# Pairwise attention scores of a four-layer graph network: ring blocks shared among three engines as a maximum

## The reference, cut to what matters

```python
s1 = jnp.einsum('bkf,ef->bke', x, W1)
s2 = jnp.einsum('bkf,ef->bke', x, W2)
pre = s1[:, :, None, :] + s2[:, None, :, :] + b_lin
h = jnp.where(pre >= 0, pre, ALPHA * pre)          # ALPHA = 0.2
e = jnp.einsum('bije,e->bij', h, a) + bias
attn = softmax(e, axis=2)
out = sigmoid(jnp.einsum('bij,bjf->bif', attn, x))
```

## Time and profile before

| | before |
|---|---|
| median of 3 executions | 6323.53 us |
| lowest, highest | 6313.05, 6334.41 us |
| span of the profiled execution | 6243.5 us |
| time of the profiled execution beside its span | not given by the page; the median is 80.0 us above the span |
| TensorE matmuls, weight loads busy | 5979.7, 2282.0 us |
| VectorE busy | 5954.0 us |
| ScalarE busy | 6039.2 us |
| GpSimd busy | 305.3 us |

### The profile page before, as it was taken

How to read it: one execution, slowest core, us unless ns; L and a number is a source line. 1 busy time by engine, 2 the same in 40 slices (tenths; PEclk the granted TensorE clock), 3 DMA queues, 4 the chain that set the end, 5 groups by cost and what they waited for, 6 DMA issues and landing times.

```text
span 6243.5 us, 130456 instructions
## 1 busy us (share of the span) xinstructions
PE 5979.7 (96%) x41684; PEld 2282.0 (37%) x41684; DVE 5954.0 (95%) x22159; ACT 6039.2 (97%) x15993; POOL 305.3 (5%) x646
## 2 busy tenths in 40 slices
PE   8899999999999999999999999999999999999997
PEld 2233333333333333333333333333333333333334
DVE  9999999999999999999999999999999999999993
ACT  8999999999999999999999999999999999999993
POOL 0000000000000000000000000000000000000000
PEclk9999999999999999999999999999999999999998
DMA  0000000000000000000000000000000000000000
GB/s 12 3 4 7 7 6 3 6 7 7 6 3 7 6 7 7 6 3 6 7 7 6 3 7 6 7 7 2 7 6 7 7 6 3 7 6 7 6 4 6
DMA packets 44317, 36.24 MB, mean 6 GB/s; under 512 B 4721, under 2 KB 39410, under 8 KB 43506
## 3 DMA queue, kind: packets, MB, share of 16 engines
q1 hardware_dynamic: 43506, 26.50, 1.4%
HBM read 9.71 MB, written 8.39 MB: 3 GB/s over the span
## 4 chain that ended last, share of the span: by engine, by line
PE 48%; ACT 41%; DVE 9%; issue 2%; POOL 1%; DMA 0%; SPq 0%; ACTq 0%; DVEq 0%; POOLq 0%
ACT ring L711 34%; PE S L912 26%; PE R L856 8%; DVE ring L514 7%; PE S L856 4%; PE V L856 3%; PE PA L856 1%; PE R L1054 1%; ACT h L753 1%; ACT cand L824 1%; ACT tz L821 1%; PE S L903 1%; PE S L906 1%; PE R L1062 1%; ACT mT L815 1%
## 5 line engine op out<-in xcount | busy, mean ns | idle before, releaser
L711 ACT ACTIVATE ring<-V,U 128x256 f32<-128x256 f32 x13472 | 5443.3, 963 | 1.3 <-DVE G L488 1.3
L514 DVE TENSOR_SCALAR ring<-V,U 128x256 f32<-128x256 f32 x19296 | 5199.2, 345 | 24.7 <-PE S L912 21.3
L912 PE MATMUL S<-ring,a_window 128*32 128x512 f32 x32768 | 3814.0, 598 | 80.3 <-ACT ring L711 52.9
L912 PEld LDWEIGHTS S<-ring,a_window 128*32 128x32 f32 x32768 | 934.7, 110 | 2432.6 <-issue 2189.1
L856 PE MATMUL R<-mT,W 128*128 128x512 f32 (+1 forms) x640 | 338.9, 611 | 2.7 <-ACT mT L815 2.7
L416 POOL TENSOR_TENSOR minus_mean<-mv,minus_one 128x4 f32<-128x4 f32 (+1 forms) x160 | 44.4, 278 | 5852.6 <-DVE mv L535 3216.6
L856 PE MATMUL R<-AT,h 128*128 128x256 f32 x1260 | 316.7, 395 | 2.7 <-ACT h L827 2.1
L856 PEld LDWEIGHTS R<-AT,h 128*128 128x128 f32 x1260 | 230.2, 193 | 129.9 <-issue 82.2
L419 POOL TENSOR_TENSOR rstd<-var,minus_half 128x4 f32<-128x4 f32 (+1 forms) x160 | 186.7, 1167 | 12.5
L856 PEld LDWEIGHTS R<-mT,W 128*128 128x128 f32 x640 | 109.2, 189 | 205.0 <-issue 181.4
L648 DVE SCALAR_TENSOR_TENSOR rh<-tr,h3T 128x512 f32<-128x512 f32 (+1 forms) x165 | 110.8, 672 | 70.4 <-ACT tr L818 70.4
(11 more groups left out here) (178 smaller groups left out, 4371.8 us busy)
## 6 DMA issues: line engine op xcount, KB each, us to landing
X<-in_x SPq DMA_DIRECT2D x64, 128.0 KB, 2.1
X_held<-X SPq DMA_DIRECT2D x32, 256.0 KB, 2.3
out<-OUT SPq DMA_DIRECT2D x64, 128.0 KB, 1.9
raw<-in_L_gnn_w_w SPq DMA_DIRECT2D x3, 128.0 KB
A<-in_adj SPq DMA_DIRECT2D x1, 256.0 KB, 2.7
Wn<-in_L_gnn_Wn SPq DMA_DIRECT2D x1, 128.0 KB
Wm<-in_L_gnn_Wm SPq DMA_DIRECT2D x1, 128.0 KB
rawu<-in_L_gnn_u_w SPq DMA_DIRECT2D x2, 64.0 KB
```

Of the source, the lines that this page charges most:

```text
L514: block_ = dve.tensor_scalar(ring[:, place, g, half * N:(half + 1) * N], V[:, y, c], U[:, y, c, i:i + 1], 0.0, ALU.add, ALU.max)
L711: last = act.activation(ring[:, place, g, half * N:(half + 1) * N], V_bank[y][:, c * N:(c + 1) * N], ACT.Relu, bias=U[:, y, c, i:i + 1])
L912: last = pe.matmul(S[y][g * ROWS:(g + 1) * ROWS, :], a_window[:, c, ROWS - 1 - row:2 * ROWS - 1 - row], ring[:, place, g], start=False, st ...
```

## The change

The rectified sum is written as a maximum. With `w = -v`, `relu(u + v) = max(u, w) - w`. VectorE and GpSimd make `max(W, U)`, ScalarE `relu(U - W)` as before with a scale of -1. Where a block was made as a maximum, the missing `-w = v` is linear, and goes into the opening matmul's weights, which now differ by column of the weights according to who makes the block.

- `AT_minus` is the negated projection matrix. The second projection now gives `W`, in a bank and a tile of that name.
- A block of VectorE is a tensor-scalar with a single `max` (line 586 of the changed kernel).
- GpSimd makes blocks too, `min` with the largest fp32 number and then `max` with the pointer, from the same `W` and `U` into the same ring (line 488). It waits for `freed` of the place as the others do, and raises `by_pool`, for which TensorE waits as a third semaphore per lot. It steps a semaphore `pool_begun` once per lot for which nobody waits.
- `share_blocks` splits a lot three ways, with 2.63, 3.57 and 4.5 for a block of VectorE, ScalarE and GpSimd, and with 20 on GpSimd for each layer norm. Per turn this gives 433 blocks to VectorE, 288 to GpSimd and 303 to ScalarE, where it was 603, 0 and 421; times 32: 13856, 9216 and 9696, where it was 19296, 0 and 13472.
- At the start GpSimd fills a mask `by_max` (one memset of 1024 columns, 75 small ones), VectorE makes from it the weights `lin_w` with two operations. The opening matmul has one weight matrix per half of the nodes: two of 256 columns in the place of one of 512.

```diff
-VECTOR_BLOCK, SCALAR_BLOCK = 2.63, 3.62
+VECTOR_BLOCK, SCALAR_BLOCK, POOL_BLOCK = 2.63, 3.57, 4.5
+LARGEST = 3.4028234e38
...
-        n = min(range(1, BLOCKS), key=lambda n: max(v + (BLOCKS - n) * VECTOR_BLOCK, s + n * SCALAR_BLOCK))
-        shares.append(n)
-        v += (BLOCKS - n) * VECTOR_BLOCK + vector[t]
-        s += n * SCALAR_BLOCK + scalar[t]
+        def ends(share):
+            d, g, a = share
+            return sorted((v + d * VECTOR_BLOCK, q + g * POOL_BLOCK, s + a * SCALAR_BLOCK), reverse=True)
+
+        d, g, a = min(((d, BLOCKS - d - a, a) for d in range(1, BLOCKS) for a in range(1, BLOCKS - d)), key=ends)
+        shares.append((d, g, a))
+        v += d * VECTOR_BLOCK + vector[t]
+        q += g * POOL_BLOCK + pool[t]
+        s += a * SCALAR_BLOCK + scalar[t]
...
+            gp.memset(by_max[:], 1.0).then_inc(mask_ones, 1)
+            gp.wait_ge(mask_ones, 1)
+            for y in range(2):
+                for c in range(EC):
+                    for n in range(BLOCKS):
+                        g, half = group_half(n)
+                        for first, end in scalar_runs(y, c, n):
+                            last = gp.memset(by_max[:, c, y, half, g * ROWS + first:g * ROWS + end], 0.0)
+            last.then_inc(mask_set, 1)
...
+            def blocks(turn, t):
+                y, p = divmod(t, LOTS_B)
+                row, c = divmod(p, EC)
+                place, rnd = t % RING, t // RING
+                d, count, _ = SHARES[t]
+
+                if p == 0:
+                    gp.wait_ge(u_ready, turn.at(2, y + 1))
+                    gp.wait_ge(w_ready, turn.at(2, y + 1))
+                need(gp, freed[place], turn.at(ROUNDS, rnd))
+                gp.sem_inc(pool_begun, 1)
+                for n in range(d, d + count):
+                    g, half = group_half(n)
+                    i = node(t, n)
+                    last = gp.tensor_scalar(ring[:, place, g, half * N:(half + 1) * N], W[:, y, c], LARGEST,
+                                            U[:, y, c, i:i + 1], ALU.min, ALU.max)
+                last.then_inc(by_pool[place], 1)
...
                 for t in range(LOTS):
                     y, p = divmod(t, LOTS_B)
+                    if turn.has_main:
+                        blocks(turn, t)
...
-                block_ = dve.tensor_scalar(ring[:, place, g, half * N:(half + 1) * N], V[:, y, c],
-                                           U[:, y, c, i:i + 1], 0.0, ALU.add, ALU.max)
+                block_ = dve.tensor_scalar(ring[:, place, g, half * N:(half + 1) * N], W[:, y, c],
+                                           U[:, y, c, i:i + 1], None, ALU.max)
...
-                    last = act.activation(ring[:, place, g, half * N:(half + 1) * N], V_bank[y][:, c * N:(c + 1) * N], ACT.Relu,
-                                          bias=U[:, y, c, i:i + 1])
+                    last = act.activation(ring[:, place, g, half * N:(half + 1) * N], W_bank[y][:, c * N:(c + 1) * N], ACT.Relu,
+                                          bias=U[:, y, c, i:i + 1], scale=-1.0)
...
-                    pe.matmul(S[y][:].rearrange("p (r j) -> p r j", r=NB), w2_lin_wide[:],
-                              H0T[:, y].unsqueeze(1).to_broadcast([P, NB, N]), start=True, stop=False,
-                              skip_group_check=True)
+                    for r in range(NB):
+                        pe.matmul(S[y][:, r * N:(r + 1) * N], lin_w[:, y, r], H0T[:, y], start=r == 0, stop=False,
+                                  skip_group_check=True)
...
                 pe.wait_ge(by_act[place], turn.at(ROUNDS, rnd + 1))
+                pe.wait_ge(by_pool[place], turn.at(ROUNDS, rnd + 1))
```

More of the change, by code:

```diff
@@ L90, in stage_costs @@
         put(scalar, PRE, half, norm=5, copy=2.6, evacuate=12)
+        put(pool, PRE, half, stats=20)
     for ln in (LN1, LN2, LN3):
@@ L134, with group_half, node, scalar_runs @@
 SPARE_BLOCKS = spare_blocks()
+def group_half(n):
+    return divmod(n, NB)
+def node(t, n):
+    row = t % LOTS_B // EC
+    g, half = group_half(n)
+    return half * P + g * ROWS + row
+def scalar_runs(y, c, n):
+    mine = [n >= BLOCKS - SHARES[y * LOTS_B + row * EC + c][2] for row in range(ROWS)]
+    edges = [row for row in range(ROWS) if mine[row] and (row == 0 or not mine[row - 1])]
+    ends = [row + 1 for row in range(ROWS) if mine[row] and (row == ROWS - 1 or not mine[row + 1])]
+    return list(zip(edges, ends))
 def gnn_stack(nc, x, adj, L0_b, L0_a, L1_Wi, L1_bi, L1_We, L1_be, L1_Wn, L1_bn, L1_Wm, L1_bm, L2_q, L2_k, L2_v,
@@ L297, in gnn_stack @@
         by_act = [sem(f"by_act{n}") for n in range(RING)]
+        by_pool = [sem(f"by_pool{n}") for n in range(RING)]
+        mask_ones, mask_set, pool_begun = sem("mask_ones"), sem("mask_set"), sem("pool_begun")
         freed = [sem(f"freed{n}") for n in range(RING)]
@@ L508, in one_block @@
                     return
[L509 removed]
+                t = lot["t"]
+                y, p = divmod(t, LOTS_B)
                 row, c = divmod(p, EC)
[L511 to L515 removed]
+                place = t % RING
+                g, half = group_half(lot["done"])
+                i = node(t, lot["done"])
+                block_ = dve.tensor_scalar(ring[:, place, g, half * N:(half + 1) * N], W[:, y, c],
+                                           U[:, y, c, i:i + 1], None, ALU.max)
                 lot["done"] += 1
@@ L707, in blocks @@
                     act.wait_ge(u_ready, turn.at(2, y + 1))
-                for n in range(BLOCKS - ACT_BLOCKS[t], BLOCKS):
-                    g, half = divmod(n, NB)
-                    i = half * P + g * ROWS + row
-                    last = act.activation(ring[:, place, g, half * N:(half + 1) * N], V_bank[y][:, c * N:(c + 1) * N], ACT.Relu,
-                                          bias=U[:, y, c, i:i + 1])
+                for n in range(BLOCKS - SHARES[t][2], BLOCKS):
+                    g, half = group_half(n)
+                    i = node(t, n)
+                    last = act.activation(ring[:, place, g, half * N:(half + 1) * N], W_bank[y][:, c * N:(c + 1) * N], ACT.Relu,
+                                          bias=U[:, y, c, i:i + 1], scale=-1.0)
                 last.then_inc(by_act[place], 1)
@@ L866, in setup_layer0 @@
                 pe.wait_ge(dve_const, DVE_CONST_A_LIN)
-                for j in range(2):
-                    for c in range(EC):
-                        mm(R1[:, j:j + 1], A[:, c, j * P:(j + 1) * P], a_lin[:, c:c + 1], c == 0, c == EC - 1)
                 for c in range(EC):
-                    last = mm(R1[:, 2:3], a_lin_wide[:, c], b0_col[:, c:c + 1], c == 0, c == EC - 1)
+                    mm(R1[:, 0:1], A[:, c, 0:P], a_lin[:, c:c + 1], c == 0, c == EC - 1)
+                for c in range(EC):
+                    mm(R1[:, 1 + c:2 + c], A[:, c, P:2 * P], a_lin[:, c:c + 1])
+                for c in range(EC):
+                    last = mm(R1[:, 3:4], a_lin_wide[:, c], b0_col[:, c:c + 1], c == 0, c == EC - 1)
                 last.then_inc(pe_const, 1)
```

101 lines of the change are left out of this document (57 added, 44 removed).

## The result

The changed kernel takes 6549.53 us (median of 4, 6545.69 to 6553.10); the kernel before, in 4 runs, 6328.97. The ratio is 1.0355 [1.0336, 1.0374]: slower by 3.5%, where 12% was forecast. The profiled execution took 6553.1 us with a span of 6551.1.

A forecast was written before the change was run, and what follows sets the result against it. VectorE, held up by GpSimd's blocks, was to set the end: 4523 us of its own work + 2488 for GpSimd's blocks + 5 at the start + 80 above the span = 7096 us, 12% slower; range 5900 to 8200.

The forecast's parts named there:

- the port: VectorE and GpSimd blocks sharing the way to SBUF: GpSimd's blocks hold VectorE up, adding 2488 us; chance 0.42.
- 0.27 us of VectorE time per GpSimd block: VectorE's charge for each of 9216 GpSimd blocks: 0.19 + 0.08 us, bounds 0 and 0.39, 2488 us in all.
- The way to SBUF: Streaming of a GpSimd block's 256 columns, during which VectorE cannot start: at least 0.19 us per block.
- the lost overlap of two VectorE blocks: VectorE's blocks around a GpSimd block no longer overlap: 345 - 263 = 82 ns, taken as 0.08 us.
- the rival at 8202: Every GpSimd block stops VectorE for its whole 0.39 us: 8202 us; whole exclusion or starvation beyond it, chance 0.08.
- The carried 80 us: Whole kernel: median of the runs, 6323.5 us, lay 80 above the profiled span; 80 was added to the forecast.
- GpSimd's block at 0.39: One ring block on GpSimd lasts 0.39 us, bounds 0.34 and 1.01; GpSimd's total 3900 us, not the bound.
- Costed at nothing: Small parts, such as the single max, ScalarE's scale, the split opening matmul and norms queued on GpSimd: 0 us.
- TensorE's floor: Rival: VectorE loses little and TensorE, at about 5820 us, sets the end; 5980 us, 5850 to 6140; chance 0.40.
- GpSimd was not the bound: Rival on GpSimd's blocks: waiting twice for the port, each takes 0.65 to 0.75 us, kernel 6841 us; chance 0.06.
- the turning point against the kernel before: VectorE's charge per GpSimd block at which the change gains nothing: (5954 - 4523) / 9216 = 0.155 us.
- no change: Rival: a charge of 0.14 to 0.17 or badly balanced shares give the gain back, about 6320 us; chance 0.04.

The follow-up runs named there:

- run 3: Changed kernel with VectorE reading its blocks' input from PSUM and ScalarE from SBUF, same shares: 6465.6 us, ratio 1.0340 to the kernel before.
- run 2: Changed kernel with GpSimd's 9216 blocks given to VectorE (23072, 0, 9696): ratio 1.1577 to the kernel before.
- run 7: Changed kernel with every block made as relu(u + v), add and max on VectorE and GpSimd, same shares: ratio 1.7592 to the kernel before.
- run 8: Changed kernel with GpSimd's min and max replaced by a single max, nothing else: ratio 1.4618 to the kernel before.
- run 1: Changed kernel without GpSimd's blocks, lots split between VectorE and ScalarE as before (19296, 0, 13472): ratio 1.0041 to the kernel before.
- run 5: Changed kernel with only new shares (10816 VectorE, 9824 GpSimd, 12128 ScalarE), planned with a charge per GpSimd block: 6139.6 us, ratio 0.9787.
- run 9: Changed kernel with VectorE reading PSUM, ScalarE SBUF, and shares from measured costs (11328 VectorE, 10752 GpSimd, 10688 ScalarE): 6056.68 us, ratio 0.9653.
- run 6: Changed kernel with half of GpSimd's blocks given to VectorE (18464 VectorE, 4608 GpSimd, 9696 ScalarE): ratio 1.0737 to the kernel before.

## Why the prediction was right, and where it was wrong

**What bounds.** Right: VectorE's blocks set the end, held up by GpSimd's blocks, which is what the prediction calls the port. With the source of VectorE's reads moved (run 3), the disturbance went on both sides. VectorE's queue holds the chain as forecast, ScalarE has over 1700 us to spare, and TensorE waits 879 us for VectorE's blocks where about 1000 was said. TensorE's busy share was to fall below 90% and stayed at 93.

**The failing step: "0.27 us of VectorE time per GpSimd block".** The runs show 0.195 on average, and a mean VectorE step of 0.395 us where 0.44 was forecast. Both parts of the term are off, and so is the count. The way to SBUF was taken at 0.19 from the affine select; in lockstep VectorE's period grows by 0.483 - 0.263 = 0.22. The second part, 0.08 for the lost overlap of two VectorE blocks, is not there: a block in lockstep is recorded 0.56 long at a period of 0.48, so neighbours still overlap by 0.08. And not every GpSimd block costs VectorE a lengthened step: 55% of 13856 blocks is some 7650 steps of about 0.48, for 9216 GpSimd blocks, which brings the average below the 0.22 of lockstep. With 0.195 VectorE's part of the sum is 4523 + 1797 = 6320, and VectorE is busy 6319.0; that the two agree is no test, since 0.195 was worked out from this busy time, but run 2 gives 0.197 by another way. The mis-sized term is worth 0.075 x 9216 = 691 us, more than the whole miss of 546.

The Trainium skill's GPSIMD Engine Reference, section "Elementwise — side-by-side cycle accounting", gives 1.03 cycles per element for a short body; at the 1.2 GHz it uses, 256 elements are an estimate of 0.22 us, and the lockstep charge is 0.22. Its 1.03 does not describe runs 7 and 8. The rule of the Trainium skill's SBUF — State Buffer, section "Who interferes with whom", that one engine holds the ports for its whole instruction, does not fit this trace, and with it falls the rival at 8202. If each engine stopped the other for its whole pace, lockstep's period would be 0.263 + 0.453 = 0.716 us, and it is 0.483. That the two take turns, one block each, the trace does bear out.

**The carried 80 us.** Wrong: the changed kernel's profiled time is 2.0 us above its span. The 80 was the difference between a span and the median of other executions. What the sum lacked instead was VectorE's idle time, 6551.1 - 6319.0 = 232 us, half of it waits for ScalarE's `tr` (115.4); 6320 + 232 is the span. The 80 and the 5 of the start hid part of it. With the right charge the prediction's own sum would have been 6320 + 85 = 6405, still 145 us short of the measured time: two errors of opposite sign stand in it, and the charge is the larger.

**GpSimd's block at 0.39.** It is 0.453 undisturbed and 0.483 in lockstep, start to start. Its place in the range was right, and it did not decide; but that a min and a max are "nearer to a select" was luck, as run 8 shows.

**Costed at nothing.** The maximum form: 0.4% in all (run 1). Setup: the first block starts at 17.01 us where it was 15.28, 1.7 us against the 5 taken. The norms: a power of four columns takes 2.82 us on average, up from 1.48, and it is up already without any GpSimd block, to 2.05 in run 1 and 2.23 in run 2 (from groups with shapes kept apart). 330.3 us of ScalarE's idle time before `h` is ended by the norms. ScalarE had over 1700 us to spare, so nothing is right as far as ScalarE goes; whether VectorE's 115.4 us of waits for `tr` come from there was not tried.

**Rivals.** TensorE's floor, held at 0.40 to come at 5980 from a charge under 0.14, is not what this kernel reached. Run 5, the same code with other shares, comes near it at 6139.6 us with 67% of the chain on TensorE, and run 9, which also moved the sources, is there at 6056.7. The floor taken at 5820 was a little low, since in run 9 TensorE is busy 5907.9. GpSimd was not the bound at 82% busy; in runs 7 and 8, with dearer operations, it was. The charge of 0.195 stands nearer to the turning point against the kernel before, 0.155, than to 0.27. That the gain is lost in the plan, since the balance counts no charge, was named in half a sentence and priced at "no change"; a new table of shares alone took the ratio from 1.0355 to 0.9787.

## What to carry to other kernels

When a planner splits work between engines, its costs must include what one engine's work costs another: here 0.2 us of VectorE for each GpSimd block left out, and 0.45 counted for a GpSimd block that takes 0.52 us in company, made a gain of 2% into a loss of 3.5% (no run parts the two). Read the pace of a stream from the timeline, at every level that it has, before and after, and not from one mean; and when two engines disturb each other, move the source of one of them, and then give the planner the new price too. Time the exact pair of operations on GpSimd before giving it a share.

## What the runs showed of the hardware that was not expected

- A GpSimd tensor-scalar of 128 x 256 fp32 takes 0.45 us with min and max (VectorE on PSUM), 0.90 to 0.93 with a single max, 1.12 to 1.14 with add and max (start to start; the last two beside VectorE blocks from SBUF).
- With both on SBUF, VectorE and GpSimd make one block each every 0.483 us (8406 of 9216 GpSimd blocks), or VectorE goes on at 0.263 while one GpSimd block lies for 5.34 us (8.09 in run 6). Both are seen with the same instructions.
- VectorE's block takes 0.392 us from PSUM and 0.263 from SBUF; ScalarE's 0.357 from PSUM and 0.399 from SBUF. The source that is slower for VectorE gives the faster kernel (run 9 against run 5).
- The price that VectorE pays depends on GpSimd's operation, and not by how long that takes: with a single max (run 8) it is (6990.8 - 879 - 3644) / 9216 = 0.27 us for each block, with the longer add and max (run 7) (6126.6 - 879 - 3644) / 9216 = 0.17. VectorE also waits for lots in both runs, which blurs the two figures a little.
